# A decoder layer on one core: the cross-attention stage in another order, its scores as 32-row tiles, and the attention loops written out

## The chip, the cores and the metric

The kernel runs on 1 core of one Trainium2 chip. The metric is the device time of one execution in microseconds, the median of several runs. TensorE's granted clock is given as a share of its full speed.

## What is computed

One decoder layer on x of 2 batches x 1024 rows x 256, in f32: self-attention, cross-attention on 77 context rows, and a mixture of 8 experts, each on a layer-normalised x and added to it. Cut to what matters here:

```python
attn = softmax(einsum("bhqd,bhkd->bhqk", q, k) * e ** -0.5) + rel_bias      # 16 heads of 16, 1024 x 1024
x = x + layernorm(attn @ v) * gamma + beta

scores = where(mask == 0, -1e9, einsum("bhsk,bhtk->bhst", q, k))            # 16 heads of 16, 1024 x 77
x = x + (softmax(scores) @ v) @ Wu + bu

topk_w, topk_idx = top_k(softmax(flat @ gate_W), 2)
out = 0.5 * gelu(flat @ shared_W + shared_b)
for e in range(8):
    out = out + combine[:, e:e + 1] * (gelu(flat @ W1[e] + b1[e]) @ W2[e] + b2[e])
x = x + layernorm(out) * gamma + beta
```

## The kernel before

Every engine has its own list of instructions, written out by hand, and semaphores tie the lists together. There is no scheduler: what stands in a list runs in that order, and a wait holds everything behind it on that engine. The 16 row tiles of 128 rows are `NT`; a chunk is four tiles, so chunks 0 and 1 are batch 0, chunks 2 and 3 batch 1. The 16 heads are four groups of four (`NG`, `HG`).

**Self-attention** (`attention`, L1489 to L1562). For each batch and group TensorE makes transposed scores in bf16 parts (L1511), ScalarE takes their exponential (L686, a loop of 8 rounds), and TensorE multiplies values as four 32-column tiles (L1489). For batch 1, TensorE (two rounds of two groups) and VectorE (four rounds) run as loops too, and batch 0's rows are finished and turned into queries beside it (L1570, L1034).

**Cross-attention.** One chunk is four groups n = 4 ch + hg. For each group:

- `scores2(ch, hg, pr)` for pr 0 and 1: two heads each. Per head one f32 matmul over all 128 rows of `k2_pad`, which holds zeros outside the head's 16 rows (L1605), and one bf16 matmul that adds the mask (L1606). Two pairs of PSUM banks take turns.
- ScalarE's exponential of a pair (L725).
- `values2(n)`: four 32-column tiles into bank 4 (L1617). `leave(n)`: VectorE copies bank 4 out (L1100). `turn2(n)`: TensorE transposes into bank 5 (L1626). `divide(n)`: VectorE divides by the sums (L1106, L1107).

After four groups a chunk's rows go on: `outputs` (TensorE transposes, L1641, ScalarE copies), `add_product` (L1649), `add_cross` (VectorE adds to x, L1117), `moments3`, `root3` (a Newton root of twelve linked operations, L814 to L820), `normalise3` (L1135), `rows3` (transposes, L1659), `shared_and_gate` (L1677, the shared expert's product and the gate's logits in one), ScalarE's copies (L709, L710), `choose` (two largest logits, L1147 to L1161), `ranks` (TensorE counts, L1690), `place` (slots, L1166 to L1178), and POOL's scatter of the rows by expert (L600, eight indirect DMAs a chunk). In the kernel before this row work of chunk ch - 1 stands inside chunk ch.

Batch 1's own rows are finished on VectorE in chunk 0 (`second_moments` to `second_normalised`), scaled by ScalarE (L731), and turned into queries by `second_columns(i)` and `second_queries(i)` at the ends of chunks 0 and 1.

A **head bound** asks before each batch whether the scores need a shift against overflow: VectorE multiplies sizes (L875), TensorE sums them by head (`head_bounds`, L1352), VectorE sets a flag (L877 to L879), and all engines read it and branch (`needed`). With this input the branch is not taken.

**Experts and end.** TensorE, VectorE and ScalarE go through 35 tiles (L1796, L1814, L1270, L762). POOL loads the weights `w2` one expert after another (L590), adds the shared bias (L605), and after ScalarE's four GELUs of the shared result (L754) halves it and adds the last bias to x:

```python
            pool.wait_ge(sg_act, NT // 4)
            nc.gpsimd.tensor_scalar(acc, acc, 0.5, None, ALU.mult).then_inc(halved, 1)
            nc.gpsimd.tensor_tensor(x_sb[:, :, :], x_sb[:, :, :], ffn_b_sb..., ALU.add).then_inc(x_shifted, 1)
```

Then it waits for the last stored results (`y_stored`) and issues 32 gathers (L622), and VectorE and ScalarE finish the rows in six rounds.

## Time and profile before

| | us |
|---|---|
| median of 3 runs (lowest, highest) | 954.3 (954.17, 956.02) |
| the profiled execution's own time | 960.4 |
| its span | 958.6, granted clock 0.923 |
| busy in the span: TensorE, VectorE, ScalarE, POOL | 795.6, 368.7, 420.2, 134.1 |

The span runs from the first to the last instruction of one execution. It has four stages: projections to 84 us, self-attention to 393, cross-attention with the routing to 603, experts to 895, and the gathering and last normalisation to the end. In a timeline row the number in brackets is the engine's idle time before the instruction, with what ended it.

### The profile page before, as it was taken

The page shows a single profiled execution, that of the slowest core. Times are in us where ns is not written, and L with a number is a line of the kernel's source. Part 1 is how long each engine was busy: PE and PEld are TensorE (multiplying, and loading weights), DVE is VectorE, ACT ScalarE, POOL GpSimd, SP SyncE. Part 2 cuts the span into 40 slices and gives each one's busy share as a digit, 9 for nine tenths or more (in the row PEclk, how much of TensorE's full clock was granted, in tenths as well). Part 3 has the DMA queues.
Part 4 walks back from the last instruction along what each step waited for, and adds up shares of the span by engine and source line. Part 5 has one row for each costly group of instructions (what it writes and reads, how often), then busy time and mean ns, then how long its engine had stood idle before and what let it go on. Part 6 is the DMA issues. An engine that isn't in the chain of part 4 may idle for free. (4 is left out here: it accounts for less than half of the span.)

```text
span 958.6 us, 12968 instructions
## 1 busy us (share of the span) xinstructions
PE 795.6 (83%) x4073; PEld 392.6 (41%) x4074; DVE 368.7 (38%) x913; ACT 420.2 (44%) x530; POOL 134.1 (14%) x113
## 2 busy tenths in 40 slices
PE   2877999999999999869989943799999999998200
PEld 1343322323222222324444432466666666665200
DVE  5792411110334344462444453133333333333265
ACT  2345689887899889333323303111111111111132
POOL 1020100010000001001041243217000000000471
PEclk9988999999999999988999965799999999999755
DMA  5859757960522500430030021775333333332243
GB/s 124 201 157 193 252 77 251 254 143 7 67 38 30 67 0 0 144 130 1 0 133 12 33 85 44 253 242 162 116 116 114 115 114 117 114 115 65 61 126 88
DMA packets 71735, 104.50 MB, mean 109 GB/s; under 512 B 9500, under 2 KB 54646, under 8 KB 71668
## 3 DMA queue, kind: packets, MB, share of 16 engines
q1 hardware_dynamic: 66444, 87.16, 34.4%
q0 software_dynamic: 5248, 16.78, 5.5%
q8 instruction: 26, 0.43, 0.2%
q14 instruction: 17, 0.14, 0.1%
HBM read 68.06 MB, written 35.85 MB: 108 GB/s over the span
## 5 line engine op out<-in xcount | busy, mean ns | idle before, releaser
L686 ACT ACTIVATE arena<-ps 128x1024 f32<-128x1024 f32 x256 | 247.8, 1022 | 46.1 <-PE ps L1511 44.6
L1511 PE MATMUL ps<-arena 99*128 99x512 bf16 x512 | 143.6, 389 | 10.5 <-issue 5.0
L1489 PE MATMUL ps<-arena 128*32 128x512 f32 x1024 | 137.2, 609 | 0.0
L1796 PE MATMUL ps<-arena 128*128 x280 | 129.6, 607 | 0.6 <-ACT arena L758 0.6
L1814 PE MATMUL ps<-arena,xh 128*128 x560 | 126.8, 379 | 1.5 <-issue 1.5
L1814 PEld LDWEIGHTS ps<-arena,xh 128*128 128x128 f32 x560 | 103.7, 190 | 14.8 <-issue 2.2
L758 ACT COPY arena<-ps 128x256 f32<-128x256 f32 x35 | 13.0, 373 | 202.1 <-PE ps L1786 202.1
L1511 PEld LDWEIGHTS ps<-arena 99*128 99x128 bf16 x512 | 36.0, 98 | 115.8 <-ACT arena L686 96.7
L1270 DVE TENSOR_TENSOR xh<-ps,xh 128x1024 f32<-128x1024 f32 x35 | 42.8, 1224 | 93.6 <-PE ps L1796 93.6
L1796 PEld LDWEIGHTS ps<-arena 128*128 128x128 f32 x280 | 51.8, 195 | 53.5 <-issue 53.4
L1605 PE MATMUL ps<-arena 128*78 128x512 f32 x128 | 69.1, 622 | 2.6 <-DVE flags L879 2.6
L725 ACT ACTIVATE arena<-ps 78x1024 f32<-78x1024 f32 x32 | 32.6, 1019 | 82.8 <-PE ps L1606 78.3
L622 POOL DMA_INDIRECT arena<-results_by_expert,slot_y x32 | 31.5, 984 | 243.1 <-DMA results_by_expert<-arena 233.6
L762 ACT ACTIVATE xh<-xh 128x1024 f32<-128x1024 f32 x35 | 37.0, 1057 | 33.8 <-DVE xh L1270 33.8
L1275 DVE COPY xh<-ps 128x1024 f32<-128x1024 f32 x35 | 42.9, 1225 | 18.9 <-PE ps L1804 18.9
L1282 DVE TENSOR_TENSOR arena<-ps,arena 128x256 f32<-128x256 f32 x35 | 14.8, 424 | 87.9 <-PE ps L1814 87.9
L600 POOL DMA_INDIRECT rows_by_expert<-xh,slot x32 | 31.0, 969 | 124.1 <-DVE slot L1173 115.6
L1489 PEld LDWEIGHTS ps<-arena 128*32 128x32 f32 x1024 | 20.3, 108 | 55.3 <-issue 53.2
L1392 PE MATMUL ps<-arena 128*128 128x512 f32 x64 | 33.5, 678 | 10.1 <-DVE arena L854 8.6
L1804 PE MATMUL ps<-ident,xh 128*128 128x128 f32 x280 | 37.3, 277 | 4.7 <-PEq L324 2.5
L1804 PEld LDWEIGHTS ps<-ident,xh 128*128 128x128 f32 x280 | 33.3, 143 | 8.6 <-issue 2.9
L1605 PEld LDWEIGHTS ps<-arena 128*78 128x78 f32 x128 | 18.2, 154 | 25.6 <-issue 23.0
(220 smaller groups left out, 776.9 us busy)
## 6 DMA issues: line engine op xcount, KB each, us to landing
xh<-in_L_ffn_b SPq DMA_DIRECT2D x35, 512.0 KB, 3.6
rows_by_expert<-arena SPq DMA_DIRECT2D x9, 1920.0 KB, 16.3
arena<-in_L_ffn_W SPq DMA_DIRECT2D x8, 1024.0 KB
arena<-in_L_ffn_W POOLq DMA_DIRECT2D x8, 1024.0 KB, 6.9
arena<-k_parts SPq DMA_DIRECT2D x48, 128.0 KB
arena<-q_parts SPq DMA_DIRECT2D x48, 128.0 KB
arena<-rows_by_expert SPq DMA_DIRECT2D x35, 128.0 KB, 2.0
arena<-in_L_ffn_b SPq DMA_DIRECT2D x35, 128.0 KB, 3.1
```

The lines of the kernel that those rows point to most:

```text
L686: nc.scalar.activation(probs[:, st % 2, h, :], ps[:, 2 * (u % 2):2 * (u % 2) + 2, :].rearrange("p a n -> p (a n)"), ACT.Exp, scale=float(D ...
L725: nc.scalar.activation(probs2[:, hg % 2, 2 * pr:2 * pr + 2, :], ps[0:CTX + 1, 2 * (u % 2):2 * (u % 2) + 2, :], ACT.Exp, scale=float(DH) ** ...
L762: nc.scalar.activation(hid, hid, ACT.Gelu).then_inc(h_act, 1)
L1270: nc.vector.tensor_tensor(hid, ps[:, 0:2, :].rearrange("p a n -> p (a n)"), b1_row[:, buf, :], ALU.add).then_inc(h_sum, 1)
L1275: nc.vector.tensor_copy(hid_t, ps[:, 4:6, :].rearrange("p a (k n) -> p (a k) n", n=P)).then_inc(ht_ready, 1)
L1392: last = nc.tensor.matmul(bank, w[:, k, P * m:P * (m + 1)], src[:, k, 512 * n:512 * (n + 1)], start=(k == 0), stop=(k == KC - 1))
L1489: last = nc.tensor.matmul(ps[32 * h:32 * h + 32, 4 + half, :], v_grp[buf][:, kt, h, :], probs[:, kt % 2, h, 512 * half:512 * (half + 1)], ...
L1511: last = nc.tensor.matmul(ps[:, 2 * (u % 2) + half, :], k_stk[buf][:, h, P * st:P * (st + 1)], q_stk[buf][:, h, 512 * half:512 * (half + 1 ...
L1605: nc.tensor.matmul(bank, k2_pad[:, b, h, :], q2_t[b][:, h // 8, at], start=True, stop=False)
L1796: last = nc.tensor.matmul(ps[:, half, :], xs_t[:, buf, k, :], w1_sb[:, bass.ds(e, 1), k, 512 * half:512 * (half + 1)].squeeze(1), start=(k ...
L1804: last = nc.tensor.transpose(ps[:, 4 + k // 4, P * (k % 4):P * (k % 4 + 1)], hid[:, P * k:P * (k + 1)], ident[:, :])
L1814: last = nc.tensor.matmul(ps[:, 6, 0:D], hid_t[:, k, :], w2_sb[:, bass.ds(e, 1), k, :].squeeze(1), start=(k == 0), stop=(k == HID // P - 1))
```

## The change

1. The loops over groups of self-attention on ScalarE, VectorE (batch 1) and TensorE (batch 1) are written out.
2. The products for batch 0's head bound are made before the last group's outputs leave; TensorE sums them right behind the last self-attention values. Batch 1's products and flag stand in chunk 1.
3. In `scores2` a matmul takes only the 32 rows that hold its head, at that row position of the array. A pair is now heads pr and pr + 2 of a group, in two different strips of 32 rows. The two mask matmuls follow.
4. Batch 1's rows are scaled and turned in chunk 1 (on ScalarE two tiles at a time). Chunk 0's row work stands in chunk 2, where chunk 1's does too; `o2` has two buffers. The ranks use other banks.
5. For chunk 3 the gate's logits get a matmul of their own (`gates`) before the shared product, and the rank stands between the two halves of that product. place(2) moves behind normalise3(3).
6. POOL adds the shared bias behind all scatters, between the weight loads. ScalarE's four GELUs of the shared result stand behind expert tiles 0 and 1 and, two of them, behind the last tile.

```diff
-                pool.wait_ge(sg_read, CHUNK * (ch + 1))
-                rows = acc[:, CHUNK * ch:CHUNK * (ch + 1), :]
-                nc.gpsimd.tensor_tensor(rows, rows, shared_b_sb.unsqueeze(1).to_broadcast([P, CHUNK, D]), ALU.add)\
-                    .then_inc(sh_added, 1)
-                if ch == NT // CHUNK - 1:
-                    for e in range(1, EXPERTS):
-                        pool.wait_ge(w2_in, 16 * e)
-                        load_w2(e)
+            pool.wait_ge(sg_read, NT)
+            for e in range(1, EXPERTS):
+                pool.wait_ge(w2_in, 16 * e)
+                if e == EXPERTS - 1:
+                    pool.wait_ge(moved_ready, 1)
+                load_w2(e)
+                if e <= NT // CHUNK:
+                    rows = acc[:, CHUNK * (e - 1):CHUNK * e, :]
+                    nc.gpsimd.tensor_tensor(rows, rows, shared_b_sb.unsqueeze(1).to_broadcast([P, CHUNK, D]), ALU.add)\
+                        .then_inc(sh_added, 1)
             pool.wait_ge(sg_act, NT // 4)
...
-            with act.Fori(0, B * NG) as g:
+            for g in range(B * NG):
...
+            def second_rows(first):
+                if first == CP:
+                    act.wait_ge(second_shift, 1)
+                for t in range(first, first + 2):
+                    nc.scalar.activation(xh[:, t, :], x_sb[:, t, :], ACT.Identity, scale=rstd[:, t:t + 1],
+                                         bias=shift[:, t:t + 1]).then_inc(second_ready, 1)
...
+            for hg in range(NG):
+                for pr in range(2):
+                    exponentials(0, hg, pr)
+            exponentials(1, 0, 0)
+            exponentials(1, 0, 1)
+            second_rows(CP)
+            exponentials(1, 1, 0)
+            second_rows(CP + 2)
+            exponentials(1, 1, 1)
+            second_rows(CP + 4)
+            second_turned(0)
+            exponentials(1, 2, 0)
+            second_rows(CP + 6)
+            second_asked(0)
+            exponentials(1, 2, 1)
+            second_turned(1)
...
             act.wait_ge(both_ready, NT // CHUNK)
             nc.scalar.activation(over[:, :], over[:, :], ACT.Exp).then_inc(pair_ready, 1)
-            for q in range(NT // 4):
+            def shared_activated(q):
                 act.wait_ge(sh_added, q + 1)
                 nc.scalar.activation(acc[:, 4 * q:4 * q + 4, :], acc[:, 4 * q:4 * q + 4, :], ACT.Gelu).then_inc(sg_act, 1)
...
             turned_rows(1, 1, 2)
             activate(1)
+            shared_activated(0)
             turned_rows(2, 0, 3)
             activate(2)
+            shared_activated(1)
...
             activate(SLOT_TILES)
+            shared_activated(2)
+            shared_activated(3)
...
-            with dve.Fori(0, NG) as g:
+            def cross_products(n):
+                link(nc.vector.tensor_reduce(size[:, :, 0], sizes[:, :, 0, 0:n], AX.X, ALU.max))
+                link(nc.vector.tensor_copy(size[:, :, 1], k2_size[:, :]))
+                bound_products()
+            for g in range(NG):
...
+                if g == NG - 1:
+                    cross_products(NG)
                 nc.vector.tensor_copy(q2_t[0][:, :, bass.ds(256 * g, 256)], pair_q).then_inc(q2_ready, 1)
                 group_outputs(1, g)
...
+                if ch < NT // CHUNK - 1:
+                    dve.wait_ge(gate_read, CHUNK * (ch + 1))
+                else:
+                    dve.wait_ge(gate_ps, 1)
+                    link(nc.vector.tensor_copy(logits, ps[:, 4, 0:CHUNK * EXPERTS].rearrange("p (t e) -> p t e", t=CHUNK)))
...
+            bound_flag(float(DH) ** -0.5, 1, 0, link)
+            shift_if_needed(0)
+            dve.wait_ge(att_done, B * NG)
+            second_moments(xh)
+            second_root(1e-3)
+            leave(0)
+            second_scaled()
+            divide(0)
+            leave(1)
+            second_added()
+            divide(1)
+            leave(2)
+            second_moments(x_sb)
+            divide(2)
+            leave(3)
+            second_root(1e-5)
+            second_normalised()
+            divide(3)
+            leave(4)
+            divide(4)
+            leave(5)
+            second_sizes(0)
+            divide(5)
+            second_sizes(1)
+            cross_products(2)
+            leave(6)
+            divide(6)
+            bound_flag(float(DH) ** -0.5, 2, 4, link)
+            add_cross(0)
+            leave(7)
+            moments3(0)
+            shift_if_needed(1)
+            divide(7)
+            root3(0)
+            normalise3(0)
+            leave(8)
+            divide(8)
+            leave(9)
+            choose(0)
+            divide(9)
+            add_cross(1)
+            moments3(1)
+            root3(1)
+            place(0)
...
+            place(0)
+            leave(10)
+            normalise3(1)
+            divide(10)
...
+            leave(15)
             divide(15)
-            place(2)
+            choose(2)
             add_cross(3)
             moments3(3)
             root3(3)
             normalise3(3)
+            place(2)
             choose(3)
             place(3)
...
-            with pe.Fori(0, NG // 2) as i:
+            for i in range(NG // 2):
                 for o in range(2):
                     attention(1, 2 * i + o, o)
             for half in range(2):
                 values(B * NG - 1, 1, NKT - 1, half)
+            head_bounds(1, 0)
...
-                    h = HG * hg + 2 * pr + hh
-                    bank = ps[0:CTX + 1, 2 * (u % 2) + hh, :]
-                    nc.tensor.matmul(bank, k2_pad[:, b, h, :], q2_t[b][:, h // 8, at], start=True, stop=False)
-                    last = nc.tensor.matmul(bank, pick[:, h, :], hide_t[0:CTX + 1 + 3 * H, 512 * ch:512 * (ch + 1)],
-                                            start=False, stop=True)
+                    h = HG * hg + pr + 2 * hh
+                    row = 32 * (h % 8 // 2)
+                    nc.tensor.matmul(ps[0:CTX + 1, 2 * (u % 2) + hh, :], k2_pad[row:row + 32, b, h, :],
+                                     q2_t[b][row:row + 32, h // 8, at], start=True, stop=False, tile_position=(row, 0))
+                for hh in range(2):
+                    last = nc.tensor.matmul(ps[0:CTX + 1, 2 * (u % 2) + hh, :], pick[:, HG * hg + pr + 2 * hh, :],
+                                            hide_t[0:CTX + 1 + 3 * H, 512 * ch:512 * (ch + 1)], start=False, stop=True)
                 last.then_inc(s2_ready, 1)
...
+            def gates(ch):
+                pe.wait_ge(x3_ready, 2 * (ch + 1))
+                pe.wait_ge(o2_out, NG * (ch + 1))
+                for t in range(CHUNK):
+                    for k in range(KC):
+                        last = nc.tensor.matmul(ps[:, 4, EXPERTS * t:EXPERTS * (t + 1)], x3_t[:, k, P * t:P * (t + 1)],
+                                                sgw_sb[:, k, D:], start=(k == 0), stop=(k == KC - 1))
+                last.then_inc(gate_ps, 1)
...
+            values2(6)
+            turn2(6)
+            pe.wait_ge(o2_out, 2 * NG - 1)
+            head_bounds(2, 4)
+            add_product(0)
+            pe.wait_ge(flag_set, 3)
+            values2(7)
+            shift_if_needed(1)
+            scores2(2, 0, 0)
+            turn2(7)
+            scores2(2, 0, 1)
+            rows3(0)
+            scores2(2, 1, 0)
+            shared_and_gate(0, 0)
+            scores2(2, 1, 1)
+            values2(8)
+            shared_and_gate(0, 1)
+            scores2(2, 2, 0)
+            turn2(8)
+            outputs(1)
+            scores2(2, 2, 1)
+            values2(9)
+            add_product(1)
+            scores2(2, 3, 0)
+            turn2(9)
+            ranks(0)
+            scores2(2, 3, 1)
+            values2(10)
+            rows3(1)
+            turn2(10)
+            shared_and_gate(1, 0)
+            values2(11)
+            shared_and_gate(1, 1)
...
+            values2(14)
+            rows3(2)
+            turn2(14)
+            shared_and_gate(2, 0)
+            values2(15)
+            shared_and_gate(2, 1)
...
             outputs(3)
             add_product(3)
+            ranks(2)
             rows3(3)
+            gates(3)
             shared_and_gate(3, 0)
+            ranks(3)
+            nc.tensor.matmul(ps[:, 4, 0:EXPERTS], ones[:, :], seen_bf[:, :], start=True, stop=False)
+            for t in range(CHUNK):
+                last = nc.tensor.matmul(ps[:, 4, 0:EXPERTS], ones[:, :], both[:, t, :], start=False, stop=(t == CHUNK - 1))
+            last.then_inc(count_ps, 1)
             shared_and_gate(3, 1)
```

**The order on TensorE in chunk 2**, where chunk 1's rows are turned (L1659 before, L1765 after). Before, from the last score pair of group 10, whose matmuls are L1605 and L1606 (L1709 and L1712 after), values are L1617 (L1723), turns L1626 (L1732):

```order
L1605 MATMUL ps<-arena 78x512 [waits s2_free]
L1606 MATMUL ps<-arena 78x512
L1605 MATMUL ps<-arena 78x512
L1606 MATMUL ps<-arena 78x512
L1617 MATMUL ps<-arena 32x512 [waits s2_free,o2_out]
L1617 MATMUL ps<-arena 32x512 x3
L1605 MATMUL ps<-arena 78x512 [waits s2_free]
L1606 MATMUL ps<-arena 78x512
L1605 MATMUL ps<-arena 78x512
L1606 MATMUL ps<-arena 78x512
L1659 MATMUL ps<-ident,xh 128x128 [waits xh_ready]
L1659 MATMUL ps<-ident,xh 128x128 x3
```

And now, from ranks(0) (L1814 to L1817):

```order
L1814 MATMUL ps<-both,before 128x32 [waits x2_added,seen_ready,both_ready]
L1816 MATMUL ps<-both,ones 128x24
L1816 MATMUL ps<-both,ones 128x16
L1816 MATMUL ps<-both,ones 128x8
L1817 MATMUL ps<-seen_bf,ones 128x32
L1709 MATMUL ps<-arena 78x512 [waits s2_free]
L1709 MATMUL ps<-arena 78x512
L1712 MATMUL ps<-arena 78x512 x2
L1723 MATMUL ps<-arena 32x512 [waits s2_free,o2_out]
L1723 MATMUL ps<-arena 32x512 x3
L1765 MATMUL ps<-ident,xh 128x128 [waits xh_ready,rank_read]
L1765 MATMUL ps<-ident,xh 128x128 x3
```

A score pair, values2(10) and the rank now stand between the product of chunk 1 and rows3(1), which also waits for the rank to be read. Before, the row work there was that of chunk 1 alone.

**The order on POOL**: scatters are L600 (L606 after), bias additions L605 (L618), weight loads L590 (L596). Before, from the third chunk's last scatters:

```order
L600 DMA rows_by_expert<-xh,slot 17280x256 [waits slot_ready]
L600 DMA rows_by_expert<-xh,slot 17280x256 x7
L605 TENSOR_TENSOR arena<-arena,rows_sb 128x1024 [waits sg_read]
L590 DMA arena<-in_L_ffn_W 128x8x256 [waits x2_added]
L600 DMA rows_by_expert<-xh,slot 17280x256 [waits slot_ready]
L600 DMA rows_by_expert<-xh,slot 17280x256 x7
L605 TENSOR_TENSOR arena<-arena,rows_sb 128x1024 [waits sg_read]
L590 DMA arena<-in_L_ffn_W 128x8x256 [waits w2_in] x7
L613 TENSOR_SCALAR arena<-arena 128x4096 [waits sg_act]
L614 TENSOR_TENSOR x_sb<-x_sb,rows_sb 128x4096
```

And now:

```order
L606 DMA rows_by_expert<-xh,slot 17280x256 [waits slot_ready]
L606 DMA rows_by_expert<-xh,slot 17280x256 x7
L596 DMA arena<-in_L_ffn_W 128x8x256 [waits x2_added]
L606 DMA rows_by_expert<-xh,slot 17280x256 [waits slot_ready]
L606 DMA rows_by_expert<-xh,slot 17280x256 x7
L596 DMA arena<-in_L_ffn_W 128x8x256 [waits w2_in,sg_read]
L618 TENSOR_TENSOR arena<-arena,rows_sb 128x1024
L596 DMA arena<-in_L_ffn_W 128x8x256 [waits w2_in]
L618 TENSOR_TENSOR arena<-arena,rows_sb 128x1024
L596 DMA arena<-in_L_ffn_W 128x8x256 [waits w2_in]
L618 TENSOR_TENSOR arena<-arena,rows_sb 128x1024
L596 DMA arena<-in_L_ffn_W 128x8x256 [waits w2_in]
```

The bias additions have left the places behind the scatters and stand between weight loads; scatters of chunks 2 and 3 have only one weight load between them.

**The order on ScalarE**: GELUs of the shared result are L754 (L812 after), expert activations L762 (L820), weighting of gathered rows L848. Before, ahead of the first expert tile:

```order
L751 ACTIVATE over<-over 128x16 [waits both_ready]
L754 ACT_TABLE_LOAD
L754 ACTIVATE arena<-arena 128x1024 [waits sh_added] x4
L758 COPY arena<-ps 128x256 [waits xs_ps] x2
L762 ACTIVATE xh<-xh 128x1024 [waits h_sum]
L758 COPY arena<-ps 128x256 [waits xs_ps]
L762 ACTIVATE xh<-xh 128x1024 [waits h_sum]
```

And now, at the last expert tile:

```order
L322 COMPARE_AND_BRANCH
L322 UNCONDITIONAL_BRANCH [waits xs_ready,h_act]
L820 ACTIVATE xh<-xh 128x1024 [waits h_sum]
L812 ACTIVATE arena<-arena 128x1024 [waits sh_added] x2
L848 ACTIVATE arena<-arena,weight 128x256 [waits weights_set,y_landed0]
L848 ACTIVATE arena<-arena,weight 128x256
```

Two of the four GELUs stand behind the last expert activation.

## Rows read from the trace of the kernel before

**Rows 1.** Self-attention: TensorE's waits (us, times, longest), and ScalarE's timeline.

```profile
PE ps L1511 <- ACT arena L686: 3.2, 9, 0.6
...
129.97 1.28 ACT L686 ACT_TABLE_LOAD   x1
```

**Rows 2.** Stretches: cross-attention and experts (us, busy and count by engine, clock, DMA).

```profile
398.00:550.50 152.50, 137.56 (x564) 65.05 (x564) 67.60 (x245) 51.48 (x82) 24.81 (x19) 0.93 0.19 70
...
604.00:894.00 290.00, 283.58 (x1184) 195.86 (x1185) 100.12 (x104) 49.78 (x70) 24.78 (x8) 0.98 0.42 135
```

**Rows 3.** Timeline of TensorE, chunk 0 (start us, us, engine, line, names, shapes, count).

```profile
407.28 1.02 PE L1605 MATMUL ps<-arena 128*78 128x512 f32 x2
408.14 0.38 PE L1606 MATMUL ps<-arena 126*78 126x512 bf16 x1
408.45 1.06 PE L1617 MATMUL ps<-arena 78*32 78x512 f32 x8
409.44 1.08 PE L1605 MATMUL ps<-arena 128*78 128x512 f32 x2
410.36 0.38 PE L1606 MATMUL ps<-arena 126*78 126x512 bf16 x1
```

**Rows 4.** Timeline of TensorE, the waits before batch 1's work.

```profile
428.75 1.97 PE L1659 MATMUL ps<-ident,xh 128*128 128x128 f32 x8 [3.94 <-ACT xh L731]
...
481.81 0.24 PE L1352 MATMUL ps<-head_rows,size_prod 128*1 128x8 f32 x4 [3.87 <-DVE size_prod L875]
483.45 1.99 PE L1605 MATMUL ps<-arena 128*78 128x512 f32 x2 [1.40 <-DVE flags L879]
```

**Rows 5.** Timeline of VectorE: moments3, root3, divide, normalise3, place.

```profile
451.94 1.40 DVE L1123 BATCH_NORM_STATS2 stats<-x_sb 128x6 f32<-128x256 f32 x4
453.37 0.38 DVE L1126 BATCH_NORM_AGGREGATE mv<-stats 128x2 f32<-128x6 f32 x4
...
455.09 0.16 DVE L814 TENSOR_SCALAR root_s<-mv 128x4 f32<-128x4 f32 x1
...
457.27 0.16 DVE L820 SCALAR_TENSOR_TENSOR rstd<-root_t,rstd 128x4 f32<-128x4 f32 x1
...
458.10 1.37 DVE L1135 TENSOR_SCALAR xh<-x_sb,mv,rstd 128x256 f32<-128x256 f32 x4
...
521.84 0.18 DVE L1166 TENSOR_TENSOR arena<-ps,route_c 128x32 f32<-128x32 f32 x1
...
523.57 0.17 DVE L1178 CAST seen_bf<-seen 128x8 bf16<-128x8 f32 x1
```

**Rows 6.** Timeline of TensorE: a product at full clock, last values, last product.

```profile
447.55 3.62 PE L1649 MATMUL ps<-arena 128*128 128x256 f32 x16
...
550.49 1.06 PE L1617 MATMUL ps<-arena 78*32 78x512 f32 x8
...
559.43 6.57 PE L1649 MATMUL ps<-arena 128*128 128x256 f32 x16 [0.68 <-ACT arena L693]
```

**Rows 7.** Timelines of VectorE and POOL, from the last add_cross to the last scatter.

```profile
566.04 0.69 DVE L1117 TENSOR_TENSOR x_sb<-ps,x_sb 128x512 f32<-128x512 f32 x1 [2.02 <-PE ps L1649]
...
568.62 1.74 DVE L814 TENSOR_SCALAR root_s<-mv 128x4 f32<-128x4 f32 x1
...
588.54 1.01 POOL L600 DMA_INDIRECT rows_by_expert<-xh,slot  x1 [17.32 <-DVE slot L1173]
...
597.46 0.96 POOL L600 DMA_INDIRECT rows_by_expert<-xh,slot  x1 [0.30 <-issue]
```

**Rows 8.** Timelines of ScalarE and POOL around the end of the experts.

```profile
886.83 1.06 ACT L762 ACTIVATE xh<-xh 128x1024 f32<-128x1024 f32 x1 [9.82 <-DVE xh L1270]
...
645.16 10.60 POOL L613 TENSOR_SCALAR arena<-arena 128x4096 f32<-128x4096 f32 x1
655.71 8.89 POOL L614 TENSOR_TENSOR x_sb<-x_sb,rows_sb 128x4096 f32<-128x4096 f32 x1
898.21 1.09 POOL L622 DMA_INDIRECT arena<-results_by_expert,slot_y  x1 [233.61 <-DMA results_by_expert<-arena]
```

370 lines of the change are left out of this document (191 added, 179 removed).

## Prediction

> **What bounds the kernel now.** I read the view of stretches first, then the waits of ScalarE and TensorE, then the timelines of all engines around the cross-attention, and last the chain that ended last. The reader is to see four things.
>
> In self-attention TensorE, not ScalarE, is the limit. ScalarE waits for score matmuls all the time, while TensorE lost only 3.2 us to ScalarE in 9 waits; some of these stand beside the 1.28 us table load that the ScalarE loop repeats in each of its 8 rounds [rows 1].
>
> In the cross-attention, from the first scores at 398.0 to the last values at 550.5, TensorE is busy 137.6 of 152.5 us at a mean clock of 0.93 [rows 2]. A pair of heads costs two f32 score matmuls and two bf16 mask matmuls. One head takes 0.86 us (407.28 to 408.14) plus 0.22 us, so a pair takes 2.16 us, and the 32 pairs 69 us, half of the stage [rows 3].
>
> The other losses there are stalls. Before 428.75 TensorE waits 3.94 us for batch 1's rows, which VectorE and ScalarE make during chunk 0, and before 481.81 and 483.45 for the head bound of batch 1 (3.87 and 1.40 us). After both it runs at its lower clock: the score pair at 483.45 has 1.99 us where 1.02 is usual [rows 3, 4]. All idle time of the stage is 15 us (152.5 less 137.6). The low clock costs some 8 us more, by my count of five pieces of the timeline against their full-speed twins.
>
> Behind the stage there is a chain with one thing at a time: last values, outputs, product, moments, gates, choice, rank, scatter, experts. The experts then run 35 tiles with TensorE full, and the end is POOL's 32 gathers, which start at 898.21 and follow each other.
>
> **The change, part by part**
>
> 1. *Loops written out.* Seven of eight table loads of 1.28 us go from ScalarE. TensorE, the limit, can win only what it waited there: between 0 and 3.2 us [rows 1]. I take -1.8, since three loads in batch 0 stand beside visible TensorE waits of some 0.6 to 0.9 us and those in batch 1 lie under the query projection.
>
> 2. *Head bound of batch 0 early.* Its three VectorE operations are removed from behind the last output of self-attention, but they now stand ahead of that output on the same engine, so both ends shift. I take -0.3.
>
> 3. *Scores as 32-row tiles.* The two heads of a pair now use different row strips and different PSUM banks, and their f32 matmuls stand next to each other. No row of before shows row tiles. The nearest is values2, four 32-column tiles: started at 408.45, the next work starts at 409.44, so four matmuls of 512 columns take 0.99 us, little more than one (0.86). Entering and leaving cost 0.09 and 0.06 more, 0.28 us in all above one matmul [rows 3]. If row tiles behave like that, a pair costs 0.86 + 0.28 + 0.44 = 1.58 us and saves 0.58. The bounds are 0.86 saved (no cost of changing tiles) and 0.28 lost (no overlap, but the change of tiling paid). I take 0.58, as the column tiles are the nearest row: 32 x 0.58 = -18.6.
> The Trainium skill says (TensorEngine Tiling (Array Packing), "Key Properties") that changing the tiling mode drains the engine, which speaks against this edit: 64 more changes. The 0.28 us above agrees that a change is not free; without any drain the term would be -27.5.
>
> 4. *New order of the stage.* Old stalls of 15 + 8 = 23 us go: batch 1's rows are spread over chunk 1, and the second head bound lies beside add_product(0). But the order makes new ones. I laid the new order out by hand with the durations of the timelines [rows 3, 5]: moments 1.8 (451.94 to 453.75), root 2.4 (twelve linked operations, 455.09 to 457.43), divide 0.7 (the gap to 458.10), normalise 1.4, place 1.9, and 0.7 for each pass over 512 PSUM columns as in [rows 7]. In chunk 0, leave(3) waits behind second_moments, about 1.7 us, and the low clock after the start and small waits for exponentials cost 3 more. In chunk 2, rows3(0) waits for divide(7), root3(0) and normalise3(0): VectorE needs 0.7 + 2.4 + 1.4 us after the flag, TensorE has one pair: 3.4 us idle. Then, behind add_product(1), TensorE holds one pair, turn2(9), ranks(0), one pair and values2(10), 4.9 us in all. VectorE must in that time do divide(9) 0.7 (after turn2(9)), add_cross(1) 1.4, moments3(1) 1.85, root3(1) 2.4, place(0) 1.9, leave(10) 0.7 and normalise3(1) 1.4: 10.3 us, started 2 us late. So ranks(0) waits 2.2 us for add_cross(1), and rows3(1) 5.5 us more. Behind TensorE's waits stand its own later scores, so ScalarE starves too. Chunk 3 adds 0.6 + 1.1 + 0.8, the second bound and leave(6) 1.5, and the lower clock after the two long stalls 4. Sum: 4.7 + 3.4 + 2.2 + 5.5 + 2.5 + 1.5 + 4 = 24, as much as before. One block, shared_and_gate(2, 1), 1.9 us, moves behind the last values. So this part gives +1 for stalls and -1.9 here.
>
> Parts 3 and 4: the last values2 start 19.5 us sooner.
>
> 5. *Last values to add_cross(3).* Before: 550.49 to 566.73 (566.04 + 0.69), 16.2 us, at the low clock after a stall behind choose(2): the product has 6.57 us where 3.62 is full speed [rows 6, 7]. Now leave(15) and turn2(15) no longer wait for choose(2), but 1.9 us of shared work stand first: 1.0 values + 1.9 + 0.6 turn + 0.9 divide + 1.0 transposes + 1.0 copies + 3.6 product + 0.7 = 10.7 us at full clock (turn, transposes and copies are estimates by the rows of like size: four turned tiles some 0.6, eight or two copies of 512 columns some 1.0), and 14.6 with the low clock, at which the product alone costs 3 us more. I take 12.5: -3.7.
>
> 6. *add_cross(3) to the last scatter's start.* Before 566.73 to 588.54, 21.8 us [rows 7]. gates(3) and choose(3) now go ahead of the shared product, so VectorE would be ready at about +15. But place(2) moved behind normalise3(3), so scatter(2) is queued on POOL just ahead: 1.9 moments + 2.4 + 1.4 + 1.6 place + 0.3 = 7.6, then 8 issues of 1.27 us (588.54 to 597.46 are seven) = 10.2, then the weight load 1.3: 19.1. So -2.7, and POOL's queue sets it. The shared bias additions leave this path.
>
> 7. *Two of the four shared GELUs move behind the last expert tile.* POOL may halve the shared result only after all four, then it adds the bias to x, and only then issues its gathers. Before, both (10.60 + 8.89 us) were done at 645 to 665, beside the experts. Now: the last ACTIVATE ends at 886.83 + 1.06 = 887.9, two GELUs of the same size, 1.06 us each, to 890.0, POOL 10.6 + 8.9 to 909.6, against a first gather at 898.21: **+11.4** [rows 8]. Everything after is paced by the gathers and moves along. The bounds are +11.4 and, if the halving ran as the two-input addition did, +9.7.
> The Trainium skill says (GPSIMD Engine Reference, "3.1 Elementwise — side-by-side cycle accounting") that a body of few operations runs at 1.03 cycles per element; at the 1.2 GHz in that section's own example 4096 elements would be an estimated 3.5 us, and the term +4.3. The row of this very instruction says 10.60, so the row decides; by the rule the time would be 7.1 us less, an estimated 930.6, and it is part of the third rival below.
>
> Sum: -1.8 - 0.3 - 18.6 + 1 - 1.9 - 3.7 - 2.7 + 11.4 = -16.6. Against the profiled execution (span 958.6, its own time 960.4) that is a span of 942. The median of the runs is 954.3, 6 us below that execution, and I move it by the same amount: **937.7 us**.
>
> **Rivals**
>
> - *Row tiles run one after the other* (slower). Then a pair costs 2.16 + 0.28 = 2.44 us, so the 32 pairs give +9.0 instead of -18.6. TensorE then has more to do inside the new stalls, which shrink by some 7. The sum is -1.8 - 0.3 + 9 - 6 - 1.9 - 3.7 - 2.7 + 11.4 = +4.0: 958.3. It turns slower once a pair costs over about 2.3 us. For it: no row shows row tiles. Against: column tiles overlap fully.
> - *The chain on VectorE binds harder.* If the low clock stays on through most of chunks 2 and 3 (the stalls of 3 to 5 us are like those that brought it down at 424 and 481 [rows 4]), another 8 us are lost: 946.
> - *The halving is quick at the end.* At the end VectorE has nothing to do beside it. The trace shows that the two engines can hold each other up: at 568.62 a VectorE operation of 0.16 us took 1.74 while POOL was adding [rows 7]. VectorE is busy a third of the expert stage [rows 2], so if every such moment stopped POOL, a third of 10.6 us would go: -3.5, which gives 934.
> - *The stalls are as short as before's smallest* and the clock stays full in the tail: 10 us less, 928.
>
> **Chances.** Forecast 0.62, with 931 to 945 as its own range; row tiles in series 0.11; VectorE binds harder 0.12; quick halving 0.05; short stalls 0.10. The range 928 to 950 leaves out the series case and a little of each end. A measurement of this kernel tells apart about 0.2%, or 1.9 us. Faster by more than that 0.87, within it 0.03, slower 0.10: the serial case is nearly all of the latter two.
>
> **What would show it.** Right: the two score matmuls of a pair begin within 0.1 us of each other, and pairs start about 1.6 us apart where nothing waits; the last values2 near 531; rows3(1) waits over 4 us for normalise3(1); POOL's halving and addition stand between the last expert tile and the first gather, 11 us late against the last store. Wrong: pairs 2.2 us or more apart; a gather less than 5 us after the last store; the last values2 later than 540.

## The result, and the profile after

The changed kernel takes **963.0 us** (median of three runs, 962.7 to 964.7; a fourth, disturbed execution is left out), where the kernel before took 954.8 (four runs beside it). The ratio of the means is 1.0089, 95% interval 1.007 to 1.0109: **slower by 0.9%**. The forecast was 937.7 us with a range of 928 to 950, so both the time and the sign are wrong.

The profiled execution took 964.7 us, with a span of 962.8 and a mean granted clock of 0.896 (before: 958.6 and 0.923). Both spans can be laid over each other at five marks. The third column applies the prediction's own terms to the marks of before.

```
mark (us)                      before   forecast   after
first score matmul             398.0    395.9      398.8
start of the last values2      550.5    528.9      557.6
first issue of scatter(3)      588.5    560.5      586.5
last expert result (L1385)     895.1    867.1      893.4
first gather                   898.2    881.6      907.7
```

At the last mark the two kernels differ by 9.5 us; the medians differ by 8.3. The spans differ by 4.2 only: in the profiled execution of before, VectorE pauses several times between 931 and 944 in the final rounds (1.58 and 2.48 us are the longest), and after's trace has no such pauses. From the first gather to the end before takes 60.4 us and after 55.1. The other runs of before are some 6 us shorter and probably lack the pauses, but no trace of them shows it.

The miss is largest at the second mark: 28.7 us, of which the first mark has 2.9. So I start there. Timeline of TensorE after, start of the stage and the query projection of batch 1 (start us, us, engine, line, operation, names, shapes, count):

```profile
398.84 2.00 PE L1709 MATMUL ps<-arena 32*78 32x512 f32 x4 [2.98 <-DVE flags L943]
400.76 1.07 PE L1712 MATMUL ps<-arena 126*78 126x512 bf16 x2
401.77 1.99 PE L1709 MATMUL ps<-arena 32*78 32x512 f32 x4
403.69 1.07 PE L1712 MATMUL ps<-arena 126*78 126x512 bf16 x2
...
453.40 4.13 PE L1831 MATMUL ps<-arena 128*128 128x512 f32 x8
457.46 1.08 PE L1709 MATMUL ps<-arena 32*78 32x512 f32 x4
```

A pair starts 2.93 us after the one before it (398.84, 401.77, ...), which is slower than before's 2.16 [rows 3]. Behind the query projection the same four records take 1.08 instead of 1.99 us. The view of stretches says why (us, busy and count of PE, PEld, DVE, ACT, POOL; then TensorE's clock, DMA share, GB/s):

```profile
404.00:414.00 10.00, 10.00 (x26) 1.63 (x24) 1.88 (x6) 3.06 (x3) 0.00 (x0) 0.50 1.02 409
414.00:424.00 10.00, 10.00 (x30) 2.84 (x29) 6.03 (x16) 2.04 (x2) 0.00 (x0) 0.50 0.26 107
424.00:434.00 10.00, 9.12 (x32) 2.45 (x33) 5.83 (x23) 2.04 (x2) 0.00 (x0) 0.50 0.00 1
434.00:444.00 10.00, 10.00 (x26) 2.52 (x22) 3.75 (x18) 3.85 (x5) 0.00 (x0) 0.50 0.01 2
444.00:454.00 10.00, 10.00 (x33) 3.95 (x30) 1.02 (x3) 5.55 (x10) 0.00 (x0) 0.50 0.00 0
```

But for one wait of 0.88 us (before 430.51) TensorE is busy all the time, and still stays at the lower of its two levels, 1.2 GHz, from 399 to 454.5. Before, it was at 2.4 GHz four microseconds after the first score.

The row tiles themselves do what the forecast assumed. Later in the stage, at full clock:

```profile
528.71 1.09 PE L1709 MATMUL ps<-arena 32*78 32x512 f32 x4
529.72 0.62 PE L1712 MATMUL ps<-arena 126*78 126x512 bf16 x2
530.28 1.09 PE L1709 MATMUL ps<-arena 32*78 32x512 f32 x4
```

530.28 less 528.71 is 1.57 us for a pair; the forecast said 1.58. The stalls of the new order came too:

```profile
483.97 1.97 PE L1765 MATMUL ps<-ident,xh 128*128 128x128 f32 x8 [4.02 <-DVE xh L1206]
510.02 0.18 PE L1814 MATMUL ps<-both,before 128*128 128x32 bf16 x1 [2.10 <-DVE x_sb L1188]
518.20 1.94 PE L1765 MATMUL ps<-ident,xh 128*128 128x128 f32 x8 [5.11 <-DVE xh L1206]
...
536.20 1.78 PE L1747 MATMUL ps<-ident,arena 128*128 128x128 f32 x8 [1.13 <-DVEq L1243]
```

rows3(0) waits 4.02 us (forecast 3.4), ranks(0) 2.10 (2.2), rows3(1) 5.11 (5.5). The stage as a whole, in the view of stretches:

```profile
398.84:557.58 158.74, 143.40 (x555) 58.87 (x555) 66.98 (x248) 51.57 (x78) 20.09 (x17) 0.74 0.19 69
```

158.74 less 143.40 leaves 15.3 us idle, where before had 14.9 [rows 2]. The idle time is as before; the mean clock is 0.74 where it was 0.93.

The tail from the last values to scatter(3) shrank from 38.0 to 28.9 us. VectorE's last add_cross answers to [rows 7]:

```profile
567.45 0.69 DVE L1188 TENSOR_TENSOR x_sb<-ps,x_sb 128x512 f32<-128x512 f32 x1 [0.96 <-PE ps L1755]
```

POOL's queue sets the tail's end, as the timeline of POOL shows (the second row is the weight load between scatter(2) and scatter(3)):

```profile
584.23 0.96 POOL L606 DMA_INDIRECT rows_by_expert<-xh,slot  x1 [0.30 <-issue]
585.19 0.97 POOL L596 DMA_DIRECT2D arena<-in_L_ffn_W  x1
586.46 1.01 POOL L606 DMA_INDIRECT rows_by_expert<-xh,slot  x1 [0.30 <-issue]
```

At the end of the experts, ScalarE, POOL and VectorE answer to [rows 8]:

```profile
885.13 1.06 ACT L820 ACTIVATE xh<-xh 128x1024 f32<-128x1024 f32 x1 [9.82 <-DVE xh L1373]
886.09 1.99 ACT L812 ACTIVATE arena<-arena 128x1024 f32<-128x1024 f32 x2
```

```profile
888.18 10.56 POOL L621 TENSOR_SCALAR arena<-arena 128x4096 f32<-128x4096 f32 x1 [243.28 <-ACT arena L812]
898.73 8.79 POOL L622 TENSOR_TENSOR x_sb<-x_sb,rows_sb 128x4096 f32<-128x4096 f32 x1
907.70 1.08 POOL L630 DMA_INDIRECT arena<-results_by_expert,slot_y  x1 [0.18 <-issue]
```

```profile
893.39 0.42 DVE L1385 TENSOR_TENSOR arena<-ps,arena 128x256 f32<-128x256 f32 x1 [3.97 <-PE ps L1992]
```

The first gather is issued 14.3 us after the last expert result starts; before it was 3.1 (895.09 to 898.21).

### The profile page after: what moved, and what is told of

The parts are those of the page before. It is cut to its first block and busy times, and to the rows that moved or that the text cites. A ratio compares the mean times of both kernels' runs of the same rounds, so it can differ in the third digit from the quotient of the medians.

```text
span 962.8 us, 12400 instructions
## 1 busy us (share of the span) xinstructions
PE 799.5 (83%) x4089; PEld 388.6 (40%) x4090; DVE 365.6 (38%) x915; ACT 411.3 (43%) x519; POOL 135.0 (14%) x113
## 5 line engine op out<-in xcount | busy, mean ns | idle before, releaser
L820 ACT ACTIVATE xh<-xh 128x1024 f32<-128x1024 f32 x35 | 37.0, 1058 | 33.3 <-DVE xh L1373 33.3
L1709 PE MATMUL ps<-arena 32*78 32x512 f32 x128 | 48.4, 842 | 3.0 <-DVE flags L943 3.0
L1385 DVE TENSOR_TENSOR arena<-ps,arena 128x256 f32<-128x256 f32 x35 | 14.9, 425 | 87.9 <-PE ps L1992 87.9
L606 POOL DMA_INDIRECT rows_by_expert<-xh,slot x32 | 31.1, 970 | 105.0 <-DVE slot L1248 96.2
L621 POOL TENSOR_SCALAR arena<-arena 128x4096 f32<-128x4096 f32 x1 | 10.6, 10562 | 243.3 <-ACT arena L812 243.3
```

The lines of the kernel that those rows point to most:

```text
L820: nc.scalar.activation(hid, hid, ACT.Gelu).then_inc(h_act, 1)
L1709: nc.tensor.matmul(ps[0:CTX + 1, 2 * (u % 2) + hh, :], k2_pad[row:row + 32, b, h, :], q2_t[b][row:row + 32, h // 8, at], start=True, stop= ...
```

## The experiments

After this reading there were two theories. **Clock theory:** 32-row score matmuls do not bring TensorE's clock up from its lower level, though the engine is full. **Rival:** the early head bound, the start of the loads or the new order does it, since these changed too. Ratios are to the kernel before, run beside each kernel on the same chip (its medians there lay between 956 and 961 us, so times are compared by these ratios). The stage runs from the first score to the start of the last values2. Time at the lower clock in it is summed from stretches of 1 us, each with twice its missing share of the clock.

**1. After, scores over 128 rows again.**

```
-  row = 32 * (h % 8 // 2)
-  nc.tensor.matmul(..., k2_pad[row:row + 32, b, h, :], q2_t[b][row:row + 32, h // 8, at], ..., tile_position=(row, 0))
+  nc.tensor.matmul(..., k2_pad[:, b, h, :], q2_t[b][:, h // 8, at], start=True, stop=False)
```

> The changed kernel with its score matmuls over all 128 rows again (same pairs of heads, same order of everything). Clock theory: the 32-row tiles are what keeps TensorE at its lower clock from 398.8 to about 455 us (57 us without an idle time over 1 us). Then the clock is up again within 5 us of the first scores, as in the kernel before, chunk 0 and half of chunk 1 gain some 22 us, and 32 pairs of 2.16 instead of 1.58 us cost up to 18.6 us, less what new stalls swallow: 955 to 966 us in all. Order theory (the new order, or the place of the first scores, keeps the clock low whatever the matmuls are): the clock stays near 0.5 up to 450 us and the kernel takes 975 us or more.

Measured: 961.0 us, ratio 1.0006 (0.9988 to 1.0025), some 8 us faster than with tiles. Its timeline of TensorE:

```profile
398.48 3.21 PE L1708 MATMUL ps<-arena 128*78 128x512 f32 x4 [2.97 <-DVE flags L943]
401.49 1.06 PE L1711 MATMUL ps<-arena 126*78 126x512 bf16 x2
402.34 1.92 PE L1708 MATMUL ps<-arena 128*78 128x512 f32 x4
404.10 0.60 PE L1711 MATMUL ps<-arena 126*78 126x512 bf16 x2
404.53 1.88 PE L1708 MATMUL ps<-arena 128*78 128x512 f32 x4
```

The first pair runs slowly, the next is at full clock, 2.19 us apart (402.34 to 404.53). The last values2 start at 547.8 instead of 557.6. The order and the early bound are the same here, so the tiles kept the clock down. In the whole stage the lower clock has 17 us here and 83 with tiles.

**2. After, the two GELUs early** (shared_activated(2) and (3) behind round 0 of ScalarE's expert loop instead of behind the last tile).

```
+  round_act(0)
+  shared_activated(2)
+  shared_activated(3)
-  with act.Fori(0, SURE) as i:
+  with act.Fori(1, SURE) as i:
       round_act(i)
   ...
-  shared_activated(2)
-  shared_activated(3)
```

> The changed kernel with the two last shared GELUs behind expert tiles 3 and 4 instead of behind the last tile (round 0 of ScalarE's loop is written out for it). Queue theory: POOL's halving and addition (10.56 + 8.79 us) leave the end, the first gather follows the last store by about 3 us, and the kernel is 11.2 us faster than the changed one: 952.7. Rival (the gathers start late for another reason, or wait for something else then): under 4 us gained, 960 or more.

Measured: 958.7 us, ratio 0.9969 (0.9955 to 0.9983), 1.2% or 11.5 us below after's. Timeline of POOL:

```profile
644.04 10.60 POOL L621 TENSOR_SCALAR arena<-arena 128x4096 f32<-128x4096 f32 x1
654.59 8.88 POOL L622 TENSOR_TENSOR x_sb<-x_sb,rows_sb 128x4096 f32<-128x4096 f32 x1
896.96 1.08 POOL L630 DMA_INDIRECT arena<-results_by_expert,slot_y  x1 [233.49 <-DMA results_by_expert<-arena]
```

The first gather follows the start of the last result (893.84) after 3.1 us again. This is term 7, by itself.

**3. Before, with row tiles only** (the same replacement in L1605, with the pairs pr and pr + 2, the mask matmuls behind both, and the exponentials' buffer order that goes with it).

> The kernel before with nothing but the score matmuls as 32-row tiles (and the pairs pr, pr + 2). Clock theory: the clock stays low from the first scores (398) at least to the full-array second queries of chunk 0, so chunk 0 loses about 8 us; the other 24 pairs save 0.58 us each where TensorE is the limit: 942 to 952 us. Order theory: the clock is up by 403 as before, all 32 pairs gain: 935 to 941 us. If row tiles cost more than they give at either clock: over 954.

Measured: 957.5 us, ratio 0.9967 (0.9955 to 0.9979). In the old order too, the pairs stand 2.93 us apart and the clock is 0.50 from 398 until the query projection at 439. Then the tiles pay: from chunk 1's first score (444.38) to the last values (546.37) it takes 102.0 us instead of 110.7. From the first score to chunk 1's it takes 46.4 us instead of 41.8. Hence a small net gain of 0.3% and no loss: the old order has 8 score pairs in the slow stretch, the new one 13.

**4. After, ScalarE's and TensorE's attention loops rolled up again.**

```
-  for g in range(B * NG):
+  with act.Fori(0, B * NG) as g:
...
-  for i in range(NG // 2):
+  with pe.Fori(0, NG // 2) as i:
```

> The changed kernel with ScalarE's and TensorE's attention loops as loops again (VectorE's stays written out). The written out loops removed 7 table loads, yet the eight groups end 1.3 us later and a group of batch 1 takes 36.5 instead of 36.2 us. If writing them out is what costs: groups of 36.2 us again and 1 to 3 us less in all, 961 to 963. If it is something else (VectorE's list, placement): groups of 36.5 us and, with the table loads back, the same or up to 2 us more.

Measured: 970.7 us, ratio 1.0106 (1.0081 to 1.013), not told apart from after's 1.0089 by their intervals. The table loads are back, one a round, and the marks do not move: first score 398.82 against 398.84, last values 558.3 against 557.6. Writing these loops out gained nothing in the end. (VectorE's list stays written out in this run.)

The traces show how. With loops, TensorE waits beside the later loads as it did before; of run 4:

```profile
133.69 0.61 PE L1614 MATMUL ps<-arena 99*128 99x512 bf16 x2 [0.57 <-ACT arena L694]
134.61 0.61 PE L1614 MATMUL ps<-arena 99*128 99x512 bf16 x2 [0.31 <-ACT arena L694]
```

There are seven such waits, 2.7 us in all, and after has none of them. What after has under ScalarE is 3.4 us at the very start, 2.93 of it in one wait before 87.49, which before has too (2.94 us before 88.29, listed under issue). The first group of batch 1 is then copied out 1.1 us sooner than with loops (transposes at 277.44 against 278.51). But the groups of batch 1 follow each other after 36.5 us (350.52 to 387.08: 36.56), and after 36.2 with loops (350.87 to 387.07), so that the last one stands at the same place again. Why a group of batch 1 takes 0.3 us longer written out was not tested.

**5. After, full rows for the first four pairs, tiles from then on** (`if u < 4:` around the two forms).

> The changed kernel with full-row score matmuls in the first four pairs of chunk 0 only (units 0 to 3), 32-row tiles from then on. The four full pairs bring the clock up by 404, as in e1. Hold theory: row tiles cannot raise the clock but keep it once it is up, as they seem to in chunks 1 to 3, so chunk 0 runs at full clock to its end and the last values come near 535 us. Fall theory: a stretch made mostly of row tiles also lets the clock fall again: it drops within chunk 0, and the last values come at 550 or later.

Measured, one execution: 958.4 us (before 961.3). Timeline of TensorE:

```profile
409.52 1.88 PE L1709 MATMUL ps<-arena 128*78 128x512 f32 x4
...
412.76 1.08 PE L1718 MATMUL ps<-arena 32*78 32x512 f32 x4
...
422.86 0.65 PE L1741 MATMUL ps<-ident,arena 128*128 128x128 f32 x4 [0.88 <-DVE arena L1171]
...
427.50 0.66 PE L1741 MATMUL ps<-ident,arena 128*128 128x128 f32 x4 [1.42 <-DVE arena L1171]
...
429.66 1.97 PE L1718 MATMUL ps<-arena 32*78 32x512 f32 x4
...
442.90 3.41 PE L1840 MATMUL ps<-arena 128*128 128x512 f32 x7
```

Four full pairs bring the clock up (1.00 from 406), and the tiles behind them run at it for some 17 us (412.8 to 429). After two short waits, 0.88 and 1.42 us, it falls, and stays down under tiles until the query projection, 13 us later. So tiles did not raise the clock here, nor bring it back. That the two waits alone made it fall is not shown: run 10 below has the same two, followed by the same tiles, and keeps its clock. The last values2 start at 546.9, between the 535 of the hold theory and the 550 of the fall theory, since the clock also falls behind the stalls of chunks 2 and 3.

**6. After, early GELUs, full rows in chunk 0 alone** (`if ch == 0:` around the two forms).

> The changed kernel with both faults that I suspect mended: the GELUs early as in e2, and full-row score matmuls in chunk 0, row tiles in chunks 1 to 3. Clock theory: chunk 0 as in e1 (batch 1's second queries start some 14 us sooner than the 453.4 of the changed kernel), 24 pairs keep their 0.58 us: the last values near 542, the ratio to the kernel before 0.983 to 0.988. Rival (the new order's own stalls swallow what the tiles give): as e1 with the early GELUs, 0.989 or more.

Measured: 942.9 us, ratio 0.9863 (0.9791 to 0.9934). Faster than both kernels. The interval is wide, with four executions between 940.3 and 954.7 us; run 10 repeats the kernel.

**7. Before, with tiles in chunks 1 to 3.**

> The kernel before with row tiles in chunks 1 to 3 and full rows in chunk 0. Clock theory: chunk 0 as in the kernel before (chunk 1's first scores at 439.8), then the 8.7 us that e3 gains between chunk 1's first scores and the last values (102.0 against 110.7 us): ratio 0.990 to 0.993. Rival (the low clock comes back in the later chunks as tiles fill them): no better than e3's 0.9967.

Measured: 954.0 us, ratio 0.9913 (0.9885 to 0.9942), 0.5% better than with tiles in all four chunks (0.9967).

**8. After, score matmuls over 64 rows** (`row = 64 * (h % 8 // 4)`, 64 rows at a tile position of 0 or 64). The rival here is that the overlap of two tiles, not their rows, keeps the clock down.

> The changed kernel with each score matmul over the 64 rows of its group of heads at row position 0 or 64, so the two of a pair share rows and cannot overlap. It asks whether the use of half the array is enough to bring the clock up. If what matters is how much of the array the matmuls fill: the clock stays low longer than with full rows, perhaps to 453. If what matters is that two tiles run side by side: the clock is up by 404 as in e1.

Measured, one execution: 1003.2 us. Timeline of TensorE:

```profile
403.47 3.69 PE L1709 MATMUL ps<-arena 64*78 64x512 f32 x4
407.10 1.07 PE L1712 MATMUL ps<-arena 126*78 126x512 bf16 x2
408.10 3.70 PE L1709 MATMUL ps<-arena 64*78 64x512 f32 x4
```

The four records take 3.7 us: nothing overlaps, and TensorE stays at 0.50 up to the query projection at 475.5. The clock stays down without any overlap, so overlap is not the cause.

**9 to 11. The order by itself, the tiles by themselves, and a later order.** Run 9 is after with full rows everywhere and early GELUs; run 10 is run 6 again; run 11 is run 10 with chunk 2 in another order:

```
 TensorE   scores2(2, 1, 0), scores2(2, 1, 1), values2(8) ahead of rows3(0)
           values2(10) ahead of ranks(0)
           scores2(3, 0, 0), values2(11), scores2(3, 0, 1) ahead of rows3(1)
 ScalarE   exponentials, turned_rows3, shared_results in the same order
 VectorE   normalise3(1) ahead of place(0)
```

> The change without its row tiles (all 32 pairs over 128 rows) and with the two GELUs behind expert tiles 3 and 4: what is left is the order, the early head bounds and the written-out loops. By the working of the prediction this should give -1.8 - 0.3 + 1 - 1.9 - 3.7 - 2.7 = -9.4 us, a ratio of 0.990; by the two runs so far (full rows 1.0006, GELUs worth 11.5 us) 0.9887. Clock theory: full rows beat after's tiles because of the clock; in chunks 1 to 3 the tiles keep the clock most of the time and save 24 x 0.58 = 14 us less some time at the lower clock, so this kernel should be 5 to 10 us slower than the one with full rows in chunk 0 alone. Rival (tiles bring nothing in chunks 1 to 3 either, because TensorE then waits for VectorE): no difference between the two.

> The kernel with full rows in chunk 0, tiles in chunks 1 to 3 and early GELUs once more, beside the two others of this call and in five rounds, since its first interval was 1.4% wide. Expected: a ratio of 0.986, and a profiled span near 940.

> The same kernel with one more change, the order of chunk 2: rows3(0) two pairs and values2(8) later, ranks(0) behind values2(10), rows3(1) behind the second pair and values2(11) of chunk 3, and on VectorE normalise3(1) ahead of place(0). In the kernel beside it TensorE waits there 4.0 (rows3(0)), 2.1 (ranks(0)) and 4.9 us (rows3(1)), and runs at its lower clock from 466 to about 473 and from 500 to 503, some 5 us more. Theory (each of these waits is lost time that the order made, part 4 of the prediction): last values some 9 to 14 us sooner, and the clock full through chunk 2. Rival (VectorE's and ScalarE's own chain sets the end, and idle time only moves to later waits such as ranks(1), outputs(2), rows3(2)): under 3 us sooner.

Measured: run 9 948.9 us, ratio 0.9875 (0.9843 to 0.9906); run 10 941.3, 0.9809 (0.9786 to 0.9831); run 11 **932.8, 0.974** (0.9711 to 0.977), the fastest kernel of this study. Run 9 is the change without tiles and without late GELUs, so the new order with the early bounds (the loops gave nothing): 1.25% of 960 is 12 us gained, where the working of the prediction gives 9.4 (0.990, inside the interval). Run 10 against run 9: the tiles in chunks 1 to 3 are worth 0.66%, some 6 us, and shorten the stage from 149.8 to 142.2 us. They could save 24 x 0.58 = 14; they also lengthen the time at the lower clock from 18 to 32 us, half of which is lost.

Run 10 also answers run 5. From 422.7 on both have the same instructions with the same two waits, but run 10 had full rows up to 420 and run 5 only up to 411. Here the tiles stay at full clock (1.09 us for the four records, where run 5 has 1.97), and the clock holds until 463:

```profile
422.66 0.66 PE L1742 MATMUL ps<-ident,arena 128*128 128x128 f32 x4 [0.88 <-DVE arena L1172]
...
427.31 0.65 PE L1742 MATMUL ps<-ident,arena 128*128 128x128 f32 x4 [1.42 <-DVE arena L1172]
...
429.46 1.09 PE L1719 MATMUL ps<-arena 32*78 32x512 f32 x4
```

So what ran before the waits counts as well; these are two executions, and no run takes it apart further. Of run 10, the long waits of TensorE:

```profile
466.57 1.97 PE L1775 MATMUL ps<-ident,xh 128*128 128x128 f32 x8 [4.02 <-DVE xh L1207]
492.38 0.18 PE L1824 MATMUL ps<-both,before 128*128 128x32 bf16 x1 [2.10 <-DVE x_sb L1189]
500.56 1.94 PE L1775 MATMUL ps<-ident,xh 128*128 128x128 f32 x8 [4.87 <-DVE xh L1207]
```

and of run 11 in the same stretch:

```profile
487.10 0.66 PE L1741 MATMUL ps<-ident,arena 128*128 128x128 f32 x4 [1.80 <-DVE arena L1171]
504.74 0.19 PE L1823 MATMUL ps<-both,before 128*128 128x32 bf16 x1 [1.45 <-issue]
```

11.0 us of waiting became 3.2 (all idle time of the stage: 16.8 us became 8.5), and the last values2 start 7.4 us sooner (532.7 against 540.1). It is under the 9 to 14 that I expected, since the lower clock did not leave: 28 us against 32; it fell at 488, right behind the wait of 1.80. Still, each microsecond of wait taken away came back as nearly one (8.5 us between the medians), so those waits were real losses and not idle time that only moves.

**12 to 14. Rows or form?** The 64-row run still had a tile position, so the tiled form could be the cause. These three have none: `k2_pad[0:n, b, h, :]`, `q2_t[b][0:n, h // 8, at]` with n of 96, 64 and 32. They leave out the scores of the heads in the other rows, so only the clock and the stage are read.

> The change with its score matmuls over rows 0 to 95 and no tile position. It leaves out the scores of the heads whose rows lie in 96 to 127, a quarter of them, so only the stage up to the last values is read. If what keeps the clock down is that few rows of the array carry the operands, 96 rows should still raise it as 128 do, within some 6 us of the first score, and the last values should come near 548. If it is the tiled form, no position is given here and the clock should rise as well, in all three kernels of this call.

> The same over rows 0 to 63, no tile position (half of the heads' scores left out). Rows theory: as with 64 rows at a tile position, the clock stays at 0.50 until the query projection of batch 1, pairs 4.63 us apart. Form theory: the clock rises within some 6 us and pairs are 2.15 us apart.

> The same over rows 0 to 31, no tile position (three quarters of the heads' scores left out). The two score matmuls of a pair now use the same rows, so they must follow each other: 4.6 us from pair to pair at the lower clock. Rows theory: the clock stays at 0.50 through chunk 0. Form theory: it rises.

Measured, one execution each: 955.7, 1017.3 and 1020.0 us (before 956.4). The stretch 414 to 424 in the three, in that order:

```profile
414.00:424.00 10.00, 9.38 (x42) 3.17 (x39) 7.29 (x19) 4.02 (x4) 0.00 (x0) 1.00 0.29 118
```

```profile
414.00:424.00 10.00, 10.00 (x20) 2.08 (x18) 2.70 (x7) 2.04 (x2) 0.00 (x0) 0.50 0.41 166
```

```profile
414.00:424.00 10.00, 10.00 (x23) 2.65 (x22) 3.99 (x10) 2.04 (x2) 0.00 (x0) 0.50 0.19 80
```

With 96 rows the clock is up after the first pair and the last values2 start at 546.2. With 64 and 32 rows it stays at 0.50 until the query projection (at 477.4 with 64 rows), and the pairs with 64 rows are 4.63 us apart (400.72 to 405.35). So in this stretch the number of rows decides, not the tiled form.

## Why the prediction was wrong

**The step that failed** is in part 4: "the low clock after the start and small waits for exponentials cost 3 more", and with it part 3's 32 x 0.58, which took every pair at full clock. I had carried over from before that the clock comes up a few microseconds after the first score, as if it depended on the engine being busy alone. It came up after 56 us, in the query projection over all 128 rows (453.40). Until then 13 of the 32 pairs ran, each in 2.93 us where the forecast had 1.58 and before 2.16. Time at the lower clock in the stage:

```
                                    lower clock (us)   stage (us)
before                                    21              152.5
after                                     83              158.7
after, full rows (run 1)                  17              149.3
before, row tiles (run 3)                 61              148.4
after, first four pairs full (run 5)      47              146.6
full rows everywhere (run 9)              18              149.8
full rows in chunk 0 (run 10)             32              142.2
the same, later order (run 11)            28              134.5
```

83 less 21 is 62 us more at half speed, worth up to 31 us of work. The stage was forecast 19.5 us shorter, with about as much loss to the lower clock as before (3 and 4 us, where I had counted 8 in before), and came out 6.3 longer, a miss of 25.8. The lower clock covers that, with some of its time falling into waits. Comparing after with run 1 gives the tiles alone: 9.4 us longer, where -18.6 was forecast, and 66 us more at the lower clock. The rest of the stage was forecast well: with full rows it is 3.2 us shorter than before, for -0.9.

Point by point:

- *Part 1, loops written out, -1.8:* worth nothing at the first score (run 4). The loads went, and with them seven waits of TensorE (2.7 us); 1.1 us of it was there at 277, and the groups of batch 1, each 0.3 us longer, took it back. The lower bound of 0 was right.
- *Part 2, early bound, -0.3:* right. From the last group's transposes to the first score it takes 11.8 us (387.08 to 398.84) where it took 12.3 (385.73 to 398.00). That the first score still came 0.8 us later and not 2.1 sooner lies ahead of it, in self-attention. Two us of it stand at 109, where TensorE waits for VectorE 2.25 us (before 1.07) and the product behind it takes 3.52 us (1.95). Run 4 has the same with its loops (2.05 and 2.94), so ScalarE's and TensorE's loops are not the cause; which edit is stays open. Executions differ by more than this: first scores of this order lie between 397.7 and 400.7 in the traces.
- *Part 3, a pair of tiles:* 1.57 us at full clock for 1.58. The overlap is there, and the rival "one after the other" fell. What the Trainium skill (TensorEngine Tiling (Array Packing), "Key Properties") says of the drain at a change of tiling mode fits with the 0.27 us that a pair of tiles takes above one full matmul and two mask matmuls, which is a small price; no run here takes it apart.
- *Part 4, stalls:* right in place and size (4.02, 2.10, 5.11 for 3.4, 2.2, 5.5; in all 15.3 us of idle time). The 4 us for the clock behind them in chunks 2 and 3 were too few: around rows3(0), rows3(1) and outputs(2) it was low for 10, 10 and 7 us, waits included.
- *Parts 5 and 6:* last values to add_cross(3) 10.6 us (forecast 12.5, before 16.2), from there to scatter(3) 18.3 (forecast 19.1), set by POOL's queue as said. Together -9.2 for -6.4. The experts bring little new: first matmul to last result took 292.1 us before and 290.6 after.
- *Part 7, two GELUs, +11.4:* +11.2 between last result and first gather, and 11.5 us by run 2. The rival "halving is quick at the end" fell: 10.56 us with 1.7 us of VectorE's work beside it, for 10.60 with 3.3 us of it beside the experts. So VectorE does not slow this instruction by anything that shows. The estimate by the cycle figure of the Trainium skill (GPSIMD Engine Reference, "3.1 Elementwise — side-by-side cycle accounting"), 3.5 us, is three times too low for it; the measurement decides.

The rival that came nearest was the second, "low clock stays on", with 8 us and a chance of 0.12. It placed the low clock in chunks 2 and 3, behind long stalls, and not in chunks 0 and 1, where TensorE has only two waits of 0.88 us. The slower side had a chance of 0.10, on a mechanism that did not occur.

The sum of what was measured: -9.2 in the tail, +11.2 from the GELUs, +0.8 at the start, +6.3 in the stage, +0.4 for the rest give 9.5 at the first gather. Without the 3 us that parts 5 and 6 gave beyond the forecast the miss would be larger still. Two edits lose in this change: the tiles in chunk 0 and the late GELUs. The order with the early bounds wins 12 us, and the tiles behind chunk 0 some 6.

## What to carry to other kernels

When an edit makes TensorE's instructions use fewer rows, do not take its clock from the trace of before: ask for each stretch how the clock gets up there, and price the stretch at both levels. Use such tiles where full-row matmuls have just brought the clock up, and full rows behind an idle stretch. The first is runs 6, 7 and 10. For the second there is a hint: behind rows3(0) the lower clock lasted 3.4 us with full rows (run 9, a wait of 2.70 us) and 10 with tiles (run 10, 4.02 us); a kernel with full pairs only behind the stalls was not run. A late dependency of one short instruction is priced by all that is queued behind it, here 19 us of POOL's work behind 2 us of ScalarE's.

## What the runs showed of the hardware

- TensorE stayed at 1.2 GHz for 56 us while busy all but 0.88 us. The Trainium skill (TensorE: Matmul & The Clock Gate, "What's actually happening") says that the clock follows how busy the engine has been. By the profile's busy share this trace disagrees: 10.00 of 10.00 us busy at 0.50. The f32 score matmuls with 32 and 64 rows, tiled or not, left the clock down, those with 96 and 128 rows raised it behind the first pair. The mask matmuls between them had 126 rows in every run and did not raise it. In the 128-row form all but 16 rows of the weights are zero, so zero weights are no hindrance. The other operand's rows hold the queries of all eight heads, and whether their content counts was not tested, nor why rows count.
- A clock that is up can stay up under 32-row tiles (17 us in run 5), with waits of 0.88 and 1.42 us among them too (run 10). With the same waits it fell in run 5, which had fewer full-row pairs before them.
- Two 32-row f32 matmuls of 512 columns at different row positions let the next work start after 1.01 us (528.71 to 529.72); one over 128 rows takes 0.86.
- A one-input POOL operation over 128x4096 f32 took 10.56 to 10.60 us, longer than the two-input addition of the same size (8.79 to 8.89). Beside the addition VectorE had no work in after and 3.8 us of it in before.
